# Graph convolution kernel: the bias of convolution 2 written into PSUM by ScalarE instead of added by TensorE

## The chip, the cores and the metric

One core of a Trainium2 chip runs the whole program. The time is the device time of one execution in microseconds; several executions are taken and their median is compared. One further execution is recorded by the hardware profiler, and every row below comes from it.

## What is computed

Three graph convolutions (GCN) over 30,000 nodes with 512 features and 30,000 edges, with layer norms, GELUs and residuals between them. Cut to what matters:

```python
h = relu(layernorm(x))                       # block 1 of the kernel
# x1 = x + L0(h):
r = h
h = gelu(layer_norm(gcn_conv(h, W1, b1), gamma1, beta1))       # convolution 1
h = layer_norm(gcn_conv(h, W2, b2), gamma2, beta2)             # convolution 2
x1 = x + gelu(h + r)
# x2 = x1 + L1(relu(layernorm(x1))):
out = x1 + gcn_conv(relu(layernorm(x1)), W3, b3)               # convolution 3

def gcn_conv(x, W, b):      # self loop added to every node, deg counts it
    # out[d] = sum over edges s->d of deg[s]^-1/2 deg[d]^-1/2 (x W)[s]  + b
```

## The kernel before

The 30,000 rows are worked on in 118 pairs of tiles (a pair is 256 rows, two tiles of 128 x 512, `j` = 0 and 1). The factor deg[s]^-1/2 is put on the rows before they are stored, and deg[d]^-1/2 is left out until later, so the bias enters each row as sqrt(deg) times b: a later layer norm or the last scaling takes the factor away again.

Block 1 counts degrees with one-hot products, normalises x, stores it to H0 and makes the index tables. Its VectorE queue is one written-out program; a ring of 14 buffers carries x in and H0 out. In it stand, for convolution 2 only: the transposed square roots of the degrees, split into a high and a low part (`sq_hi`, L432 to L434) and stored by SyncE to a table `SQ` in HBM (L286), and the operand `B3`, which holds b2 split the same way (L542 to L545). Tiles `root` of zeros, filled by GpSimd, are also the source of the zero rows written to H1 (L290).

Each convolution is one block that runs all pairs: the first four written out, then a hardware loop over four pairs a turn, then the last ones written out. Each engine has a `body(p, known)` that sets the order of its own queue; engines meet by semaphores. For a pair in convolution 2:

- SyncE: `load_self` (L797), `load_root` (L805, 3 rows of `SQ` for the pair), `load_x` (L817), `store_x` (L824, waits for `x2_sum`), `store_h` (L834, waits for `relu_x2`). The queue is in order: while it waits for `relu_x2`, the loads of the next body stand behind it.
- GpSimd: `residual` (L925), the gathers (L889), `power` (L932).
- TensorE: `aggregate(p+1)`: 8 transposes of the own rows (L1252), 8 of the gathered rows (L1259), 8 products of 256 columns (L1266); then `multiply_second(p)`: two bias products `root` x `B3` of 512 columns that open the two banks `Out` (L1296), and 24 products of 512 columns (L1275). The bias products wait for `cg_done` of two pairs before, that is until VectorE has read the banks (`centre`, L1117).
- VectorE: `over_low` (L1078, L1080), `low` (L1086, waits for ScalarE's `high`), `stats` of both tiles (L1094, each waits for its last product), mean and variance (L1103, L1110), `centre` (L1117), `x2_sum` of the pair before (L1144, waits for `relu_x2` of two pairs earlier, among others), `x2_mean` (L1152), `x2_scale` (L1165), `normal` (L1132), `x2_shift` (L1172), and in the loop the indices (L1072).
- ScalarE: `squares` (L1011, waits for `x2_mean`), `high` (L963), `gelu` (L979), `relu_x2` (L1021), `relu_x` (L1002, waits for the load of x), `over_high` (L957).

Convolutions 1 and 3 have no bias product. There ScalarE's `seed` (L972) writes sqrt(deg) times the bias into the bank, and `multiply` (TensorE) waits for `seeded` and then adds its products onto it.

Of the kernel before, what the change touches and what calls it, by code (L numbers as in the profile page):

```python
# [5 lines left out]
P = 128  # L6
ALU = mybir.AluOpType
ACT = mybir.ActivationFunctionType
F32 = mybir.dt.float32
# [46 lines left out]
def gnn_kernel(nc, x, src, dst, W1, b1, g1, be1, W2, b2, g2, be2, W3, b3, out):  # L56
# [19 lines left out]
    with ExitStack() as ctx:  # L76
# [45 lines left out]
        SQ = scratch("SQ", (NTE, 3 * P))  # L122
# [16 lines left out]
        sq_hi = sb("sq_hi", [P, 2, 3, P], F32R)  # L139
        B3 = sb("B3", [P, D], F32R)  # L140
# [23 lines left out]
        root = [sb(f"root{u}", [P, 2, P], F32R) for u in range(4)]  # L164
# [20 lines left out]
        b_hi, b_lo = Vhi[0][0:3, :], scratch_f[0:3, 4 * D:5 * D]  # L185
# [32 lines left out]
        roots, roots_turned, roots_made, roots_out = sem("roots"), sem("roots_turned"), sem("roots_made"), sem("roots_out")  # L218
# [29 lines left out]
        with nc.Block() as block:  # L248
            @block.sync
            def _(sp):  # L250
# [57 lines left out]
                sp.wait_ge(roots_out, 16 * len(THALF))  # L308
# [8 lines left out]
            def _(pool):  # L317
# [6 lines left out]
                for b in (B3, *(r[:, :, :] for r in root)):  # L324
                    nc.gpsimd.memset(b[...].bitcast(F32), 0.0).then_inc(consts, 1)
# [42 lines left out]
            def _(dve):  # L368
# [55 lines left out]
                nc.vector.tensor_tensor(sqrt_deg[:, :], deg1[:, :], dinv[:, :], ALU.mult).then_inc(roots, 1)  # L424
# [329 lines left out]
        def convolution(q):  # L754
# [30 lines left out]
            with nc.Block() as block:  # L785
                @block.sync
                def _(sp):
# [574 lines left out]
```

## Time and profile before

| | us |
|---|---|
| median of 3 runs | 3256.65 (3255.61 to 3258.55) |
| the profiled execution | 3256.22 |
| its span, first to last instruction | 3254.4 |
| TensorE busy in the span | 2927.4 (90%) |
| VectorE | 2558.2 (79%) |
| GpSimd | 2042.1 (63%) |
| ScalarE | 1917.1 (59%) |
| DMA, mean rate | 274 GB/s |

The profile names engines PE (TensorE matmul), PEld (its weight load), DVE (VectorE), ACT (ScalarE), POOL (GpSimd) and SP (SyncE). A trailing q is the engine's sequencer, which issues DMAs and waits. In the timeline a row is: start, length, engine, line, operation, output<-inputs, number of instructions merged, and in square brackets the idle time before it with what ended it. Instructions on one engine overlap a little, so a row's length is more than what it takes from the queue. The picture in slices of the page shows where the stages lie: block 1 to about 430 us, convolution 1 to about 1320, convolution 2 from there to about 2350, convolution 3 to the end.

### The profile page before, as it was taken

How to read it: one execution, taken by the hardware profiler on the slowest of the kernel's cores; microseconds unless marked ns; L12 is line 12 of the kernel's file. 1: busy time of each engine (PE TensorE's matmuls, PEld its weight loads, DVE VectorE, ACT ScalarE, POOL GpSimd, SP SyncE). 2: the span in 40 equal slices, each digit the busy share in tenths (PEclk: the TensorE clock that was granted, in tenths of full speed). 3: DMA queues.
4: the chain of work that ended last, by engine and by line, in shares of the span. 5: the costliest groups of instructions: out<-in, count | busy, mean ns of one | idle time of the engine just before them, and what ended most of it. 6: DMA issues, size and time to landing. Idle time of an engine off the chain costs nothing. (4 is left out here: it accounts for less than half of the span.)

```text
span 3254.4 us, 60981 instructions
## 1 busy us (share of the span) xinstructions
PE 2927.4 (90%) x16665; PEld 2468.1 (76%) x16665; DVE 2558.2 (79%) x6385; ACT 1917.1 (59%) x2847; POOL 2042.1 (63%) x1619
## 2 busy tenths in 40 slices
PE   8223359999999999899999999999969999999999
PEld 2122248888888888688888888888758888888888
DVE  9899968888888888699999999999934454454444
ACT  0256547767766776477777877777733333333333
POOL 0122257777777776588888888888655555555553
PEclk9999999999999999899999999999989999999999
DMA  3499987788888776699999999999789999999996
GB/s 130 157 355 418 416 253 213 213 216 219 214 216 218 214 215 175 225 322 331 323 328 328 322 331 323 327 326 326 262 236 287 287 289 291 285 288 287 288 289 208
DMA packets 306303, 890.91 MB, mean 274 GB/s; under 512 B 67591, under 2 KB 69033, under 8 KB 306248
## 3 DMA queue, kind: packets, MB, share of 16 engines
q1 hardware_dynamic: 190408, 682.26, 59.5%
q0 software_dynamic: 115840, 208.01, 27.1%
q8 instruction: 23, 0.38, 0.0%
q14 instruction: 32, 0.26, 0.0%
HBM read 653.10 MB, written 308.07 MB: 295 GB/s over the span
## 5 line engine op out<-in xcount | busy, mean ns | idle before, releaser
L889 POOL DMA_INDIRECT gathered<-H,idx x826 | 1154.7, 1398 | 517.0 <-issue 244.8
L1275 PE MATMUL out<-Whi,ahi 128*128 128x512 f32 x2832 | 765.6, 392 | 0.0
L1275 PE MATMUL out<-Wlo,ahi 128*128 128x512 f32 x2832 | 759.0, 390 | 0.0
L1275 PE MATMUL out<-Whi,alo 128*128 128x512 f32 x2832 | 739.3, 390 | 0.1
L963 ACT ACTIVATE ahi<-agg 128x1024 fp32r<-128x1024 f32 x354 | 361.0, 1020 | 642.1 <-PE agg L1266 586.4
L1275 PEld LDWEIGHTS out<-Wlo,ahi 128*128 128x128 f32 x2832 | 531.9, 188 | 115.7
L1275 PEld LDWEIGHTS out<-Whi,alo 128*128 128x128 f32 x2832 | 531.5, 188 | 110.9 <-DVE alo L1086 0.5
L1275 PEld LDWEIGHTS out<-Whi,ahi 128*128 128x128 f32 x2832 | 517.7, 189 | 97.3
L1078 DVE TENSOR_TENSOR vlo<-gathered,vhi 128x512 fp32r<-128x512 f32 x354 | 243.1, 687 | 320.7 <-ACT vhi L957 209.6
L1086 DVE TENSOR_TENSOR alo<-agg,ahi 128x1024 fp32r<-128x1024 f32 x354 | 429.7, 1214 | 24.0 <-ACT ahi L963 17.5
L1252 PE MATMUL agg<-ident,gathered 128*128 128x128 f32 x2832 | 370.0, 274 | 58.8 <-DMA gathered<-H,idx 49.0
L1094 DVE BATCH_NORM_STATS2 small<-out 128x6 f32<-128x512 f32 x472 | 327.0, 694 | 110.4 <-PE out L1275 77.1
L1252 PEld LDWEIGHTS agg<-ident,gathered 128*128 128x128 f32 x2832 | 331.9, 140 | 106.3 <-DMA gathered<-H,idx 50.7
L1266 PE MATMUL agg<-sv,vhi 128*128 128x256 f32 x1416 | 385.5, 305 | 1.7 <-DVE sv L1080 1.3
L925 POOL TENSOR_TENSOR r<-r,vec 128x512 f32<-128x512 f32 x236 | 298.8, 1286 | 99.3 <-DVE sv L1080 92.4
L1266 PE MATMUL agg<-sv,vlo 128*128 128x256 f32 x1416 | 356.5, 284 | 0.0
L979 ACT ACTIVATE y<-y 128x1024 f32<-128x1024 f32 x236 | 248.7, 1054 | 166.7 <-DVE y L1132 140.2
L1117 DVE SCALAR_TENSOR_TENSOR conv<-out,small,vec 128x512 f32<-128x512 f32 x472 | 331.3, 744 | 0.0
L972 ACT ACTIVATE out<-vec,sqrt_deg 128x512 f32<-128x512 f32 x472 | 306.0, 684 | 12.8 <-PEq L248 6.4
L932 POOL TENSOR_TENSOR small<-small,neg_half 128x2 f32<-128x2 f32 (+1 forms) x238 | 211.7, 889 | 151.9 <-DVE small L1110 140.2
L1181 DVE SCALAR_TENSOR_TENSOR conv<-out,dinv,x 128x512 f32<-128x512 f32 x236 | 176.6, 749 | 138.8 <-PE out L1275 119.7
L1266 PEld LDWEIGHTS agg<-sv,vhi 128*128 128x128 f32 x1416 | 272.7, 193 | 2.3 <-DVE vlo L1078 1.7
(176 smaller groups left out, 3824.2 us busy)
## 6 DMA issues: line engine op xcount, KB each, us to landing
gathered<-H SPq DMA_DIRECT2D x351, 512.0 KB
H<-ho SPq DMA_DIRECT2D x250, 512.0 KB, 9.5
x<-in_x_dram SPq DMA_DIRECT2D x165, 512.0 KB, 8.8
X<-x SPq DMA_DIRECT2D x117, 512.0 KB
x<-X SPq DMA_DIRECT2D x117, 512.0 KB
out_dram<-conv SPq DMA_DIRECT2D x117, 512.0 KB
H<-x SPq DMA_DIRECT2D x48, 512.0 KB, 9.6
gathered<-H,idx POOLq DMA_INDIRECT x826
```

Of the source, the lines that this page charges most:

```text
L889: pool.indirect_dma_start(rows, None, H[q][0:end, :], bass.IndirectOffsetOnAxis(ap=idx[p.slot(4)][:, c:c + 1], axis=0), bounds_check=end - ...
L925: nc.gpsimd.tensor_tensor(R[:, j, :], R[:, j, :], beta_b[1][:, :], ALU.add)\
L963: nc.scalar.activation(Ahi[p.slot(2)][:, :], Agg[p.slot(2)][:, :], ACT.Copy)\
L972: nc.scalar.activation(Out[2 * p.slot(2) + j][:, :], bias_b[q][:, :], ACT.Copy, scale=sqrt_deg[:, bass.ds(p.n * 2 + j, 1)]).then_inc(seede ...
L979: nc.scalar.activation(y, y, ACT.Gelu).then_inc(gelu_done.sem, 1)
L1078: nc.vector.tensor_tensor(Vlo[p.slot(2)][:, :], V[p.slot(4)][:, :], Vhi[p.slot(2)][:, :].bitcast(F32), ALU.subtract).then_inc(vlo_done.sem, 1)
L1086: nc.vector.tensor_tensor(Alo[p.slot(2)][:, :], Agg[p.slot(2)][:, :], Ahi[p.slot(2)][:, :].bitcast(F32), ALU.subtract).then_inc(lo_done.se ...
L1094: s = nc.vector.bn_stats(m[:, 6 * j:6 * j + 6], Out[2 * p.slot(2) + j][:, :])
L1117: nc.vector.scalar_tensor_tensor(CvP[p.slot(2)][:, j, :], Out[2 * p.slot(2) + j][:, :], m[:, 12 + 2 * j:13 + 2 * j], gamma_b[q][:, :], ALU ...
L1252: nc.tensor.matmul(agg[:, (2 * f + j) * P:(2 * f + j + 1) * P], own[:, j, fs], ident[:, :], is_transpose=True, start=(f % 2 == 0 and j == ...
L1266: m = nc.tensor.matmul(agg[:, 2 * f * P:2 * (f + 1) * P], part[p.slot(2)][:, f * P:(f + 1) * P], Sv[p.slot(2)][:, :], start=False, stop=(p ...
L1275: m = nc.tensor.matmul(Out[2 * p.slot(2) + j][:, :], a[p.slot(2)][:, c:c + P], w[q][:, f, :], start=False, stop=stop and f == KD - 1, skip ...
```

## The change

Convolution 2 gets its bias as the other two do: ScalarE's `seed` writes sqrt(deg) times b2 into both banks `Out` of a pair, and the two bias products are gone. `seed(p+2)` stands in ScalarE's body between `gelu(p)` and `relu_x2(p-2)`; the first two pairs are seeded ahead of the loop. TensorE waits for `seeded` (after its wait for `high`) in place of `cg_done` and of the root load. With the products go `B3`, `sq_hi`, the table `SQ`, its two stores and its 118 loads, the two transposes that turned the roots, and 12 small VectorE instructions in block 1. The zero rows of H1 come from a tile of their own, `zeros`.

```diff
-                nc.vector.tensor_scalar(row[:, 1:2], row[:, 0:1], 1.0, None, ALU.is_equal).then_inc(cols, 1)
-                dve.wait_ge(cols, 3)
-                link(nc.vector.tensor_scalar(row[:, 2:3], row[:, 1:2], -1.0, 1.0, ALU.mult, ALU.add))
...
-                sp.wait_ge(roots_made, 1)
-                for h, rows in THALF:
-                    sp.dma_start(SQ[h * P:h * P + rows, :], sq_hi[0:rows, h, :, :].bitcast(F32)
-                                 .rearrange("p a j -> p (a j)")).then_inc(roots_out, 16)
-                sp.wait_ge(consts, 6)
+                sp.wait_ge(consts, 2)
                 for k in range(2):
                     sp.dma_start(H[1][N:N + P, k * 2 * P:(k + 1) * 2 * P],
-                                 root[k][:, :, :].bitcast(F32).rearrange("p a j -> p (a j)")).then_inc(zero_out, 16)
+                                 zeros[:, :]).then_inc(zero_out, 16)
...
-                dve.wait_ge(roots_turned, 1)
-                for h, rows in THALF:
-                    r = slice(0, rows)
-                    nc.vector.tensor_copy(sq_hi[r, h, 0, :], bank[6 + h][r, 0:P])
-                    link(nc.vector.tensor_copy(sq_hi[r, h, 1, :], bank[6 + h][r, 0:P]))
-                    c = nc.vector.tensor_tensor(sq_hi[r, h, 2, :], bank[6 + h][r, 0:P], sq_hi[r, h, 0, :].bitcast(F32),
-                                                ALU.subtract)
-                c.then_inc(roots_made, 1)
...
-                dve.wait_ge(vectors_in, 16 * 7)
-                dve.wait_ge(consts, 6)
-                b = bias_b[1][0:3, :]
-                link(nc.vector.tensor_copy(b_hi, b))
-                link(nc.vector.tensor_tensor(b_lo, b, b_hi.bitcast(F32), ALU.subtract))
-                link(nc.vector.tensor_scalar(b_lo, b_lo, row[0:3, 1:2], None, ALU.mult))
-                link(nc.vector.scalar_tensor_tensor(B3[0:3, :], b_hi.bitcast(F32), row[0:3, 2:3], b_lo,
-                                                    ALU.mult, ALU.add))
...
-                pe.wait_ge(roots, 1)
-                for h, rows in THALF:
-                    m = nc.tensor.transpose(bank[6 + h][0:rows, 0:P], sqrt_deg[:, h * P:h * P + rows], ident[:, :])
-                m.then_inc(roots_turned, 1)
...
-                    def load_root(known, p, k):
-                        if not second:
-                            return
-                        if has(known, k - 4):
-                            sp.wait_ge(main_done.sem, main_done.upto(p.after(-4)))
-                        sp.dma_start(root[p.slot(4)][0:3, :, :].bitcast(F32), SQ[bass.ds(p.n * 2, 2), :]
-                                     .rearrange("o (a j) -> a o j", a=3)).then_inc(root_in.of(p), 16)
...
                         if has(known, 5):
                             load_self(known, p.after(5), 5)
-                        if has(known, 3):
-                            load_root(known, p.after(3), 3)
                         if has(known, 2):
                             load_x(known, p.after(2), 2)
...
                     def body(p, known):
                         if known == 0:
-                            if not second:
-                                seed(0, p)
+                            seed(0, p)
                             over_high(p)
...
                                 over_high(p.after(3))
+                                seed(1, p.after(1))
...
                             if has(known, 0):
                                 gelu(p)
+                            if has(known, 2):
+                                seed(of(known, 2), p.after(2))
                             if has(known, -2):
                                 relu_x2(of(known, -2), p.after(-2))
...
                     def multiply_second(p, known):
 
-                        pe.wait_ge(root_in.of(p), root_in.upto(p))
-                        for j in range(2):
-                            if known is None or known >= 2:
-                                pe.wait_ge(cg_done.sem, cg_done.upto(p.after(-2), j + 1))
-                            nc.tensor.matmul(Out[2 * p.slot(2) + j][:, :], root[p.slot(4)][:, j, :], B3[:, :],
-                                             start=True, stop=False, skip_group_check=True)
                         pe.wait_ge(hi_done.sem, hi_done.upto(p))
                         for j in range(2):
+                            pe.wait_ge(seeded.sem, seeded.upto(p, j + 1))
                             product(p, j, Ahi, Whi)
                             product(p, j, Ahi, Wlo)
```

ScalarE's queue in convolution 2, the last pair written out ahead of the loop, from `squares` to `over_high`. Before:

```order
L1011 ACTIVATE y,small<-x,small 128x512 x2
L963 ACTIVATE ahi<-agg 128x1024
L979 ACTIVATE y<-y 128x1024
L1021 ACTIVATE ho<-x,small 128x512 x2
L1002 ACTIVATE r<-x,nb_x,rstd_x 128x512 x2
L957 ACTIVATE vhi<-gathered 128x512
```

and now:

```order
L962 ACTIVATE y,small<-x,small 128x512 x2
L914 ACTIVATE ahi<-agg 128x1024
L930 ACTIVATE y<-y 128x1024
L923 ACTIVATE out<-vec,sqrt_deg 128x512 x2
L972 ACTIVATE ho<-x,small 128x512 x2
L953 ACTIVATE r<-x,nb_x,rstd_x 128x512 x2
L908 ACTIVATE vhi<-gathered 128x512
```

Two instructions more stand between `gelu` (L979, now L930) and `relu_x2` (L1021, now L972); all that follows them in the queue moves behind them.

SyncE's queue in convolution 2, the last body written out ahead of the loop: own rows, roots, x, the store of X2 and the store of H2. Before:

```order
L797 DMA gathered<-H 128x1024
L805 DMA root<-SQ 3x2x128
L817 DMA x<-in_x_dram 128x1024
L824 DMA X<-x 128x1024
L834 DMA H<-ho 128x1024
```

and now:

```order
L762 DMA gathered<-H 128x1024
L774 DMA x<-in_x_dram 128x1024
L781 DMA X<-x 128x1024
L791 DMA H<-ho 128x1024
```

The load of x now stands directly behind the load of the own rows; the waits between them are the same.

## Rows read from the trace of the kernel before

**Rows 1.** The page: busy time of each engine, its share of the span, instructions

```profile
PE 2927.4 (90%) x16665; PEld 2468.1 (76%) x16665; DVE 2558.2 (79%) x6385; ACT 1917.1 (59%) x2847; POOL 2042.1 (63%) x1619
```

**Rows 2.** Busy by stretch: stretch, length, busy (instructions) by engine, granted clock, DMA

```profile
200.00:400.00 200.00, 66.88 (x870) 45.77 (x870) 195.26 (x784) 121.06 (x167) 44.91 (x41) 1.00 1.02 415
...
1300.00:1400.00 100.00, 84.32 (x466) 73.01 (x464) 71.74 (x168) 53.46 (x81) 62.65 (x56) 0.90 0.72 241
...
1600.00:1800.00 200.00, 200.00 (x1157) 174.33 (x1156) 191.04 (x488) 158.49 (x257) 165.44 (x139) 1.00 0.94 326
```

**Rows 3.** Timeline of TensorE in convolution 2: bias products and those after

```profile
1700.73 0.63 PE L1296 MATMUL out<-B,root 128*128 128x512 f32 x2
1701.19 1.09 PE L1275 MATMUL out<-Whi,ahi 128*128 128x512 f32 x4
...
1709.37 0.63 PE L1296 MATMUL out<-B,root 128*128 128x512 f32 x2
```

**Rows 4.** Timeline of VectorE: `stats` of the first pair, then of two later ones

```profile
1344.12 1.28 DVE L1094 BATCH_NORM_STATS2 small<-out 128x6 f32<-128x512 f32 x2
...
1706.11 1.45 DVE L1094 BATCH_NORM_STATS2 small<-out 128x6 f32<-128x512 f32 x2
...
1714.64 0.69 DVE L1094 BATCH_NORM_STATS2 small<-out 128x6 f32<-128x512 f32 x1
1715.51 0.70 DVE L1094 BATCH_NORM_STATS2 small<-out 128x6 f32<-128x512 f32 x1 [0.18 <-PE out L1275]
```

**Rows 5.** Waits of ScalarE between 1450 and 2250 us: total, times, longest

```profile
ACT y L1011 <- DVE small L1152: 115.6, 89, 2.0
ACT r L1002 <- DMA x<-in_x_dram: 44.2, 69, 1.6
```

**Rows 6.** Timeline of ScalarE: a `seed` of convolution 1, a pair of convolution 2

```profile
1295.46 1.30 ACT L972 ACTIVATE out<-vec,sqrt_deg 128x512 f32<-128x512 f32 x2
...
1709.22 0.62 ACT L957 ACTIVATE vhi<-gathered 128x512 fp32r<-128x512 f32 x1
1711.03 0.72 ACT L1011 ACTIVATE y<-x,small 128x512 f32<-128x512 f32 x1 [1.19 <-DVE small L1152]
...
1714.31 1.51 ACT L1021 ACTIVATE ho<-x,small 128x512 f32<-128x512 f32 x2
1716.04 1.52 ACT L1002 ACTIVATE r<-x,nb_x,rstd_x 128x512 f32<-128x512 f32 x2 [0.22 <-DMA x<-in_x_dram]
```

**Rows 7.** Timeline: `relu_x2`, SyncE's loads behind it, `x2_sum`

```profile
1705.79 1.51 ACT L1021 ACTIVATE ho<-x,small 128x512 f32<-128x512 f32 x2
...
1708.68 0.29 SPq L805 DMA_DIRECT2D root<-SQ  x1
...
1709.24 0.32 SPq L817 DMA_DIRECT2D x<-in_x_dram  x1
...
1709.50 0.68 DVE L1144 SCALAR_TENSOR_TENSOR x<-x,y 128x512 f32<-128x512 f32 x1
```

**Rows 8.** Timeline: a late load of x, with the `relu_x2` ahead of it

```profile
1515.63 1.50 ACT L1021 ACTIVATE ho<-x,small 128x512 f32<-128x512 f32 x2
...
1519.88 0.33 SPq L817 DMA_DIRECT2D x<-in_x_dram  x1
...
1526.97 1.52 ACT L1002 ACTIVATE r<-x,nb_x,rstd_x 128x512 f32<-128x512 f32 x2 [1.21 <-DMA x<-in_x_dram]
```

**Rows 9.** Timeline of VectorE in block 1: around `sq_hi`, around `B3`

```profile
105.87 0.29 DVE L432 CAST sq_hi<-out 128x128 fp32r<-128x128 f32 x1 [0.37 <-PE out L607]
...
107.32 2.46 DVE L444 BATCH_NORM_STATS2 x_st<-conv 128x6 f32<-128x512 f32 x4
...
163.95 0.41 DVE L542 CAST vhi<-vec 3x512 fp32r<-3x512 f32 x1
...
166.40 2.47 DVE L444 BATCH_NORM_STATS2 x_st<-conv 128x6 f32<-128x512 f32 x4
```

**Rows 10.** Timeline of TensorE: transposes after a long idle time, before convolution 2

```profile
1322.36 1.97 PE L1252 MATMUL agg<-ident,gathered 128*128 128x128 f32 x8 [9.73 <-PEq L785]
```

More of the change, by code:

```diff
@@ L121, in gnn_kernel @@
         DST = scratch("dst_padded", (PADDED, 1), I32)
-        SQ = scratch("SQ", (NTE, 3 * P))
         ident = sb("ident", [P, P])
@@ L138, in gnn_kernel @@
         rstd_x, nb_x = sb("rstd_x", [P, NTE]), sb("nb_x", [P, NTE])
-        sq_hi = sb("sq_hi", [P, 2, 3, P], F32R)
-        B3 = sb("B3", [P, D], F32R)
         sqrt_deg = sb("sqrt_deg", [P, NTE])
@@ L163, in gnn_kernel @@
         idx = [sb(f"idx{u}", [P, 3], I32) for u in range(4)]
-        root = [sb(f"root{u}", [P, 2, P], F32R) for u in range(4)]
+        zeros = sb("zeros", [P, 2 * P])
         small = [sb(f"small{u}", [P, 36]) for u in range(4)]
@@ L184, in gnn_kernel @@
         fl = scratch_f[:, 3 * D:4 * D].rearrange("p (h j) -> p h j", h=2)
-        b_hi, b_lo = Vhi[0][0:3, :], scratch_f[0:3, 4 * D:5 * D]
         lo_t = sb("lo_t", [P, NC])
@@ L217, in gnn_kernel @@
         place_made, place_used = sem("places_made"), sem("places_used")
-        roots, roots_turned, roots_made, roots_out = sem("roots"), sem("roots_turned"), sem("roots_made"), sem("roots_out")
         w_split, w_free = sem("weights_split"), sem("weights_staged_free")
@@ L307, in _ @@
                     sp.dma_start(SelfP[n], whole(H[0], n, False)).then_inc(self_in.of(Pair(0, n)), 16)
-                sp.wait_ge(roots_out, 16 * len(THALF))
                 sp.wait_ge(vectors_in, 16 * 7)
@@ L323, in _ @@
                     nc.gpsimd.memset(m[:, :], 1.0)
-                for b in (B3, *(r[:, :, :] for r in root)):
-                    nc.gpsimd.memset(b[...].bitcast(F32), 0.0).then_inc(consts, 1)
+                nc.gpsimd.memset(zeros[:, :], 0.0).then_inc(consts, 1)
                 pool.wait_ge(padded, 48)
@@ L423, in _ @@
                 nc.vector.tensor_scalar(eps2[:, :], deg1[:, :], EPS, None, ALU.mult)
-                nc.vector.tensor_tensor(sqrt_deg[:, :], deg1[:, :], dinv[:, :], ALU.mult).then_inc(roots, 1)
+                nc.vector.tensor_tensor(sqrt_deg[:, :], deg1[:, :], dinv[:, :], ALU.mult)
                 dve.wait_ge(pair_cnts, 1)
@@ L740, in gnn_kernel @@
         g_self = sem("g_self")
-        root_in, xt_in = Landed("root_in", 4), Landed("xt_in", 4)
+        xt_in = Landed("xt_in", 4)
         ho_out, xo_out = Landed("ho_out", 2), Landed("xo_out", 2)
@@ L851, in fetch_x @@
                                 sp.wait_ge(xo_out.of(p), xo_out.upto(p))
-                            else:
-                                sp.dma_start(root[n][0:3, :, :].bitcast(F32), SQ[2 * n:2 * n + 2, :]
-                                             .rearrange("o (a j) -> a o j", a=3)).then_inc(root_in.of(p), 16)
                             sp.dma_start(XtP[n][:, :, :], whole(X2 if second else x, n, False)).then_inc(xt_in.of(p), 16)
@@ L860, in body @@
                                 load_self(0, p.after(k), k)
-                            load_root(0, p.after(2), 2)
                             load_self(0, p.after(4), 4)
@@ L1319, in convolution @@
             if second:
-                root_in.close()
                 for flag in (r_done, rb_done, x2_done, mean2_done, sq2_done, sc2_done, co2_done):
                     flag.close()
-            else:
-                seeded.close()
+            seeded.close()
             if third:
```

## The prediction

> **What bounds the kernel now.** I read the busy line of the page first, then the busy times by stretch, then the timeline of the engines in convolution 2, then the waits of ScalarE. TensorE is busy for 90% of the span [rows 1], and for all of the middle stretch of convolution 2 [rows 2]: 200.00 of 200.00 us. But there VectorE is busy for 191.04 of the same 200 us, and the DMA for 0.94 of them, so whatever TensorE gives back is capped soon. The pace of convolution 2 is TensorE's: from the bias products of one pair to those of the next 1709.37 - 1700.73 = 8.64 us [rows 3]. Of these the two bias products take 1701.19 - 1700.73 = 0.46 us; their row is 0.63 long because a matmul overlaps the next.
>
> How much slack has VectorE? It meets TensorE in one place, `stats`, which waits for the last products. In the first pair, where the products were long done, its two instructions took 1.28 us; later 1.45, and 1715.51 + 0.70 - 1714.64 = 1.57 [rows 4]. So VectorE waits for TensorE 0.17 to 0.29 us a pair, I take 0.22. Its own pace is then 8.64 - 0.22 = 8.42 us.
>
> ScalarE's slack: between 1450 and 2250 us, that is in 92.6 pairs, it waits 115.6 us for `x2_mean` and 44.2 us for the load of x [rows 5], 1.73 us a pair. Its own string is 8.64 - 1.73 = 6.91 us.
>
> **What the change does, part by part.**
>
> TensorE, convolution 2: two products fewer, 0.46 us a pair, pace 8.64 - 0.46 = 8.18 us. If TensorE stayed the bound, 118 x 0.46 = 54 us. It doesn't: VectorE's 8.42 is longer. So the most that a pair can give is 0.22 us, by the two ends of rows 4 0.17 to 0.29, times 117 steps 20 to 34 us, at 0.22 26 us.
>
> ScalarE, convolution 2: two `seed` instructions a pair. In convolution 1 such two take 1.30 us, the overlap with the next about 0.1, so 1.20 [rows 6]. ScalarE's string becomes 6.91 + 1.20 = 8.11 us, 0.31 under VectorE's 8.42. That is little. The Trainium skill (ScalarE: Activation LUTs, "Step-by-step: what each stage is for") says that ScalarE writes faster into PSUM than into SBUF. The rows don't agree: a 512-wide copy into SBUF takes 0.62, and of two seeds into PSUM each 0.65 or more. By the page the two seeds would cost at most 2 x 0.62 - 0.1 = 1.14, and the slack would be 0.37 in place of 0.31; the time would be some 1 us lower.
>
> The new wait, TensorE for `seeded`: queued behind it are the 24 products of the pair, and for those wait `stats` and all behind it. The seeds of a pair are issued where `relu_x2` starts now, 1714.31 [rows 6], and end 1.3 us later, 1715.6. The products of their pair follow the bias products at 1709.37 + 8.64 = 1718.01 [rows 3]. 2.4 us to spare, so this wait costs nothing in the loop. At the start the seeds stand in ScalarE's idle time before the first gather has landed, nothing either.
>
> What stands behind the seeds in ScalarE's queue: `relu_x2` is done 1.20 later. Two wait for it. VectorE's `x2_sum` starts at 1709.50, the `relu_x2` it needs ends at 1705.79 + 1.51 = 1707.30 [rows 7]: of 2.20 us 1.00 is left, 0.8 at the faster pace. And SyncE's store and, behind it, the next load of x.
>
> **The loop through the load of x** is the part that decides. From the end of `relu_x2` 1707.30 SyncE issues the store, the own rows, the roots (1708.68), and at 1709.24 x; `relu_x` starts at 1716.04 after a wait for it [rows 6, 7]. That is 8.74 us after the end of `relu_x2`, 6.80 of it from issue to use. In a late case `relu_x2` ends at 1517.13, x is issued at 1519.88 and used at 1526.97: 9.84 us, 7.09 from its issue [rows 8]. On the mean ScalarE waits 44.2 / 92.6 = 0.48 us there [rows 5], so x comes about 8.64 + 0.48 = 9.12 after `relu_x2`. Without the root load the issue is 1709.24 - 1708.68 = 0.56 earlier: 8.56 on the mean, 9.28 in the late case. From the start of `relu_x` to the end of the `relu_x2` that closes the loop, ScalarE needs `relu_x` and `over_high`, 1.52 + 0.62 less overlaps = 2.0, from `squares` to the end of `relu_x2` 1714.31 + 1.51 - 1711.03 = 4.79, and now 1.20 for the seeds: 8.0 us. The loop spans two pairs. On the mean it takes 8.56 + 8.0 = 16.56, 8.28 a pair, under VectorE's 8.42. In a late case 17.28, which is 0.44 over two of VectorE's pairs. Reading along the timeline, about one load in four is late like this. When it is, `squares` starts late, then `high`, then VectorE's `low`: I take 0.3 us for one pair in four, 0.08 a pair. Pace 8.50.
>
> 117 x (8.64 - 8.50) = 16.4 us gained in convolution 2.
>
> Block 1: `sq_hi` holds VectorE from 105.87, after a wait of 0.37, to 107.32, 1.8 us; `B3` from 163.95 to 166.40, 2.45 us [rows 9]. VectorE is busy 195.26 of the 200 us that follow [rows 2], so both lie on the path; against it, the DMA share there is 1.02. Bounds 0 and 4.3, I take 4, nearer to VectorE's row. The stores of `SQ` and the memsets of `root` go from queues that wait there anyway: nothing. Convolution 3 and convolution 1 are as they were: nothing.
>
> Sum: 16.4 + 4 = 20.4 us. The profiled execution took 3256.22 and becomes 3235.8; the median of the runs is 0.4 above it, so 3236.
>
> **The rivals.** *VectorE's pace in full*: no late load is felt, 8.42 to 8.35 a pair. 26 to 34 us and 4.3: 3226 down to 3218. For it: the root loads are off the queue; against it the thin slack of ScalarE. Its upper part belongs to my case.
>
> *ScalarE takes TensorE's place*: late loads are the rule, 17.28 / 2 = 8.64 a pair. Nothing is gained in convolution 2, and 0 to 4 in block 1: 3252 to 3257. For it: ScalarE's slack falls from 1.73 to 0.3 us, and at a quicker pace the DMA, at 0.94, is pressed harder. Against it: the same DMA moves 415 GB/s in block 1 and 326 here [rows 2].
>
> *Slower, the load of x comes later still*: with `relu_x2` later, x falls into the gathers of GpSimd. The loop is longer than 2 x 8.64 as soon as x takes 17.28 - 8.0 = 9.28 us after `relu_x2` on the mean and not 8.56, 0.72 more. If it took 1.2 us more, (9.76 + 8.0) / 2 = 8.88 a pair, 117 x 0.24 = 28 us lost, 4 gained: 3280.
>
> *Slower by the clock*: after 9.73 idle us eight transposes took 1.97 us [rows 10], and the granted clock of that stretch is 0.90, a mix of 1.2 and 2.4 GHz [rows 2]. In convolution 2 TensorE would idle 8.50 - 8.18 = 0.32 us a pair, which it does not now. At 1.2 GHz a pair would need 16.4 us, so 6% of the time at that clock is enough to be slower than now; 15% would be 8.18 x 1.15 = 9.4 a pair, +89 us, 3342. Against it: in block 1 TensorE is busy 66.88 of 200 us at a clock of 1.00 [rows 2]. The Trainium skill (TensorE: Matmul & The Clock Gate, "A second HAM failure mode: psum-queue depth-cycling") warns of such short idle times between groups of matmuls; by block 1 they do no harm here.
>
> *The change doesn't do what it says*: VectorE turns out faster than I read and the full 54 us come: 3198.
>
> **How the numbers follow.** Chances: my case, 3226 to 3249, 0.60; VectorE's pace in full, 0.12; the full 54 us 0.02; ScalarE in TensorE's place 0.16, of it 0.02 still faster; the load of x 0.07; the clock 0.01; something in the start or the end of a block that I don't see, 0.02, slower. About 0.2%, 6.5 us, is what a measurement of this kernel can tell from no change. Faster 0.76, same 0.14, slower 0.10. Predicted 3236; the range for 8 in 10 goes from 3222, inside VectorE's pace in full, to 3257, where nothing is gained.
>
> **What would show it.** Right: no L1296; the pace of convolution 2 between 8.42 and 8.60; VectorE's `stats` back at 1.28 us with no wait for TensorE; TensorE idle about 0.3 us a pair, in front of the products or of the transposes; ScalarE's wait for `x2_mean` fallen from 1.25 to some tenths, at times none; block 1 some 4 us shorter. Wrong: VectorE's `low` waiting for `high` in most pairs (ScalarE is the bound); x used more than 7.6 us after its issue; a granted clock under 1.00 between 1400 and 2300; convolution 1 or 3 changed in length.

## The result, and the profile after

| | before | after |
|---|---|---|
| median of 6 runs each, us | 3256.2 (3254.8 to 3258.6) | 3271.7 (3266.3 to 3275.2) |
| ratio, with its 95% interval | | 1.0046 (1.0036 to 1.0057) |
| span of the profiled execution | 3254.4 | 3270.8 |
| first to last product of convolution 1 | 859.0 | 858.3 |
| first to last product of convolution 2 | 1013.8 | 1032.6 |
| first to last product of convolution 3 | 858.4 | 858.1 |

The forecast was 3236 and faster; the kernel is 15 us slower. Convolution 1 begins 2.5 us earlier, convolutions 1 and 3 take what they took, and convolution 2 takes 18.8 us more. Here and below the pace of convolution 2 is the mean distance between the starts of VectorE's first `centre` of one pair and of the next, over some 90 pairs between 1440 and 2250 us. It was 8.64 us before, the same as in [rows 3], and is 8.83 after.

The busy line of the page after, to be read beside [rows 1]:

```profile
PE 2904.5 (89%) x16427; PEld 2433.2 (74%) x16427; DVE 2548.5 (78%) x6373; ACT 2053.4 (63%) x3083; POOL 2062.6 (63%) x1615
```

and the stretch from the middle of convolution 2, with the columns of [rows 2] (busy us and instructions of PE, PEld, DVE, ACT, POOL, then clock, DMA share, GB/s):

```profile
1600.00:1800.00 200.00, 190.61 (x1083) 162.92 (x1082) 185.57 (x474) 179.60 (x294) 165.85 (x135) 0.99 0.94 317
```

TensorE was busy for 200.00 of these 200 us and is now for 190.61; VectorE fell from 191.04 to 185.57, and the DMA from 326 to 317 GB/s. ScalarE rose from 158.49 to 179.60 and isn't full either; GpSimd stayed where it was (165.44, now 165.85). No engine is the bound: a chain that passes through several of them is. The waits between 1450 and 2250 us (total us, times, longest) name it:

```profile
ACT r L953 <- DMA x<-in_x_dram: 64.4, 64, 2.8
...
PE out L1228 <- ACT out L923: 31.2, 44, 1.6
DVE alo L1039 <- ACT ahi L914: 26.3, 41, 1.4
...
ACT y L962 <- DVE small L1105: 11.6, 28, 0.7
```

Beside [rows 5]: ScalarE's wait for `x2_mean`, its slack, fell from 115.6 to 11.6 us. Its wait for the load of x rose from 44.2 to 64.4, and there are two waits that were not there before: TensorE waits for the seeds, and VectorE's `low` for ScalarE's `high`. VectorE waits for TensorE nowhere, so its `stats` are back at the length that [rows 4] shows for the first pair, as forecast.

One turn of the chain, from the timeline of ScalarE and of SyncE's queue (start, length, engine, line, operation):

```profile
1701.68 1.51 ACT L972 ACTIVATE ho<-x,small 128x512 f32<-128x512 f32 x2
...
1703.36 0.35 SPq L791 DMA_DIRECT2D H<-ho  x1
...
1704.12 0.35 SPq L762 DMA_DIRECT2D gathered<-H  x1
...
1704.78 0.34 SPq L774 DMA_DIRECT2D x<-in_x_dram  x1
...
1712.68 1.52 ACT L953 ACTIVATE r<-x,nb_x,rstd_x 128x512 f32<-128x512 f32 x2 [0.27 <-DMA x<-in_x_dram]
...
1718.03 1.29 ACT L923 ACTIVATE out<-vec,sqrt_deg 128x512 f32<-128x512 f32 x2
1719.26 1.51 ACT L972 ACTIVATE ho<-x,small 128x512 f32<-128x512 f32 x2
```

`relu_x2` ends at 1703.19. SyncE issues the store, the own rows, and at 1704.78 the load of x. `relu_x` had to wait for it and starts at 1712.68, 9.49 us after the end of `relu_x2` and 7.90 after the issue. The `relu_x2` that ends this turn is done at 1720.77, 8.09 later: 17.58 us for two pairs, 8.79 a pair. On the mean of the stretch x is issued 1.54 us after the end of `relu_x2` and used 7.99 after that, 9.53 together. With ScalarE's 8.0 us that is 17.53, 8.77 a pair.

What a late x does to the others stands in two rows of the same pair, VectorE's `low` and TensorE's first products:

```profile
1699.64 1.22 DVE L1039 TENSOR_TENSOR alo<-agg,ahi 128x1024 fp32r<-128x1024 f32 x1 [1.36 <-ACT ahi L914]
...
1701.18 1.19 PE L1228 MATMUL out<-Whi,ahi 128*128 128x512 f32 x4 [1.46 <-ACT out L923]
```

### The profile page after: what moved, and what is told of

Its sections match the earlier page's. It is cut to its first block and busy times, and to the rows that moved or that the text cites. A ratio compares the mean times of both kernels' runs of the same rounds, so it can differ in the third digit from the quotient of the medians.

```text
span 3270.8 us, 60605 instructions
## 1 busy us (share of the span) xinstructions
PE 2904.5 (89%) x16427; PEld 2433.2 (74%) x16427; DVE 2548.5 (78%) x6373; ACT 2053.4 (63%) x3083; POOL 2062.6 (63%) x1615
## 5 line engine op out<-in xcount | busy, mean ns | idle before, releaser
L1228 PE MATMUL out<-Whi,ahi 128*128 128x512 f32 x2832 | 778.9, 397 | 39.8 <-ACT out L923 38.5
L1228 PEld LDWEIGHTS out<-Whi,ahi 128*128 128x128 f32 x2832 | 509.9, 189 | 146.0 <-ACT out L923 50.9
L923 ACT ACTIVATE out<-vec,sqrt_deg 128x512 f32<-128x512 f32 x708 | 458.0, 681 | 16.4 <-PEq L750 9.8
L1047 DVE BATCH_NORM_STATS2 small<-out 128x6 f32<-128x512 f32 x472 | 315.2, 688 | 99.0 <-PE out L1228 99.0
L930 ACT ACTIVATE y<-y 128x1024 f32<-128x1024 f32 x236 | 248.8, 1054 | 163.0 <-DVE y L1085 162.9
```

The source lines that it names most:

```text
L923: nc.scalar.activation(Out[2 * p.slot(2) + j][:, :], bias_b[q][:, :], ACT.Copy, scale=sqrt_deg[:, bass.ds(p.n * 2 + j, 1)]).then_inc(seede ...
L930: nc.scalar.activation(y, y, ACT.Gelu).then_inc(gelu_done.sem, 1)
L1047: s = nc.vector.bn_stats(m[:, 6 * j:6 * j + 6], Out[2 * p.slot(2) + j][:, :])
L1228: m = nc.tensor.matmul(Out[2 * p.slot(2) + j][:, :], a[p.slot(2)][:, c:c + P], w[q][:, f, :], start=False, stop=stop and f == KD - 1, skip ...
```

## The experiments

**Is it the loop through the load of x? Open it, before and after.** The first two runs load x a body earlier, in the changed kernel and in the kernel before (this edit and those below are for convolution 2 alone):

```diff
                         if has(known, 5):
                             load_self(known, p.after(5), 5)
-                        if has(known, 2):
+                        if second and known == 0:
+                            load_x(0, p.after(2), 2)
+                        if not second and has(known, 2):
                             load_x(known, p.after(2), 2)
...
                         if has(known, -1):
                             store_x(known, p.after(-1), -1)
+                        if second and has(known, 3):
+                            load_x(known, p.after(3), 3)
                         if has(known, -lag):
                             store_h(known, p.after(-lag), -lag)
```

> The changed kernel with one reorder in SyncE's queue of convolution 2: the load of x for the next body but two is issued right behind the store of X2, ahead of the store of H2, so that it no longer waits for relu_x2. Theory A (the loop relu_x2 -> store -> load of x -> relu_x -> relu_x2 sets the pace of 8.83 us): the loop is cut, VectorE's own 8.42 to 8.45 us becomes the pace, 117 x 0.39 = 46 us less than the changed kernel's 3271.7, so 3224 to 3229, clearly under the kernel before; ScalarE doesn't wait for x. Theory B (ScalarE's own string with the seeds is too long): no gain from the reorder, 3268 to 3273. Theory C (TensorE's new wait for the seeds, or its clock): no gain either.

> The kernel before with the same reorder of the load of x. Theory A: TensorE sets the pace there (8.64 us), the wait for x was covered, so 3256 within 2 us; only ScalarE's wait for x goes and its wait for x2_mean grows by as much. If the load of x had cost something before too, it would be faster.

Measured: e1 3241.7 us, ratio to before 0.9957 (0.994 to 0.9973), pace 8.57. e2 3255.6, 1.0001 (0.9991 to 1.001), pace 8.64. The same edit takes 30 us from the changed kernel and nothing from the one before. ScalarE's wait for x is gone from the waits of e1. So waiting behind the load of x is what makes the changed kernel slow, and it cost the one before nothing. e2 came as forecast; e1 missed its 3224 to 3229 by 13 us, for it stops at 8.57 and not at the 8.42 of the prediction. That is the second question, taken up below.

**Or get `relu_x2` out of the seeds' way, or x out of the own rows' way.** e3 keeps all loads where they are and moves the seeds behind `relu_x2`:

```diff
                             if has(known, 0):
                                 gelu(p)
+                            if has(known, -2):
+                                relu_x2(of(known, -2), p.after(-2))
                             if has(known, 2):
                                 seed(of(known, 2), p.after(2))
-                            if has(known, -2):
-                                relu_x2(of(known, -2), p.after(-2))
```

> The changed kernel with seed(p+2) behind relu_x2(p-2) in ScalarE's queue and not ahead of it; SyncE's order as in the change. The seeds then fill the time in which ScalarE waits for the load of x. Theory A (the loop through the load of x): the seeds are out of the loop, 9.5 + 6.8 us in two pairs, so VectorE's 8.57 is the pace: 3241 to 3244, as the two kernels at 3241. Theory B (it is the sum of ScalarE's work that is too much): the sum is the same, so 3268 to 3274. Against A as far as TensorE needs the seeds: they end 1.5 us later, of 2.4 us that there were.

e6 issues the load of x ahead of that of the own rows:

```diff
+                        if second and has(known, 2):
+                            load_x(known, p.after(2), 2)
                         if has(known, 5):
                             load_self(known, p.after(5), 5)
-                        if has(known, 2):
+                        if not second and has(known, 2):
                             load_x(known, p.after(2), 2)
```

> The changed kernel with the load of x ahead of the load of the own rows in SyncE's queue of convolution 2; it still stands behind the store of H2. A dose between the change and the load ahead of that store. Theory A: x is issued 0.7 us earlier and with 512 KB less ahead of it, which is worth 1.5 us or more of the 9.5 after relu_x2: the loop falls under two of VectorE's pairs, pace 8.57, 3241 to 3245. If x comes when it came, whatever the order of issue, 3268 to 3274.

Measured: e3 3239.6 us, 0.9955 (0.9938 to 0.9971); e6 3241.4, 0.9955 (0.9939 to 0.9972). e6 lies in its forecast and e3 1.4 us under its own. Three different ways to shorten the loop, one place where they stop. In e3 the seeds run while ScalarE waits for x anyway, so they cost nothing. In e6 x is used 8.47 us after `relu_x2` and not 9.53, and in only one of 94 pairs does ScalarE still wait for it.

**Both remedies together.**

> The changed kernel with both remedies of the first runs: the load of x a body earlier, and the seeds behind relu_x2. Theory L (the loop through the load of x sets the changed kernel's pace, and behind it stands VectorE's own pace of 8.57 us): either remedy alone already reaches VectorE's pace, so both together give no more than one: 3239 to 3242 us, pace 8.55 to 8.57. Rival S (each remedy takes a share of a cost of its own): 3239.6 less some 10 us, under 3232.

3241.2 us, 0.9957 (0.994 to 0.9973), pace 8.56: no more than one alone.

**The seeds alone, and no bias at all.** e4 is the kernel before with the seeds added: the bias products stay and open the banks, which discards what the seeds wrote, and TensorE waits for the seeds. e5 is the changed kernel without seeds and without b2; the first product of a tile opens its bank.

> The kernel before with ScalarE's two seeds a pair added in convolution 2, in the place where the change has them, and nothing taken away: the bias products stay and overwrite the seeds, and wait for them. Theory A (the delay of relu_x2 by 1.2 us is the whole cause): the pace is 8.8 us or, since the root load still stands ahead of the load of x, up to 9.1; with block 1 as before 3256 + 117 x (0.2 to 0.45) = 3279 to 3308. Theory C (TensorE loses its full load, its clock or its start-up after a wait): TensorE still has all its products, so close to 3256.

> The changed kernel with no bias at all in convolution 2: neither seeds nor bias products, the first product opens the bank. b2 is left out of the result. This is the saving alone, without its price. Theory A: ScalarE is as it was, TensorE at 8.18 us, so VectorE's 8.42 is the pace: 3256.2 - 117 x 0.22 - 2.5 (block 1) = 3228. If VectorE's own pace was misread, it shows here: 3200 if TensorE stays the bound, 3250 or more if something else is.

e4: 3269.6 us, 1.0048 (1.0031 to 1.0064), pace 8.73. e5: 3241.3, 0.9958 (0.9941 to 0.9974), pace 8.57. Neither came as forecast. e4 lies between the 3256 of theory C and the 3279 from which theory A began: the seeds alone do make the kernel before slower, and there x comes 9.32 us after `relu_x2`, which by the loop is (9.32 + 8.0) / 2 = 8.66 a pair. e5 stops at 8.57 like e1 and not at 8.42. Seen from e5, the change is a gain of 15 us, for the products and all that came with them, and a loss of 30 us for the seeds where they stand.

**The dose.** e9 writes one seed a pair (tile 1 gets no bias), e11 writes a third tile between the two seeds, into SBUF, for nobody. e12 is e11 with the load of x a body earlier.

```diff
                         for j in range(2):
+                            if second and j == 1:
+                                if known is None or known >= 1:
+                                    act.wait_ge(third_done.sem, third_done.upto(p.after(-1)))
+                                nc.scalar.activation(extra[:, :], bias_b[q][:, :], ACT.Copy)\
+                                    .then_inc(third_done.sem, 1)
```

> Half the dose: in convolution 2 only tile 0 of a pair is seeded, tile 1 has no bias (b2 is left out of it) and its first product opens the bank. Theory L: ScalarE's part of the loop is 8.0 - 0.6 = 7.4 us, x comes 9.2 to 9.5 us after relu_x2, so the loop is 16.6 to 16.9 over two pairs, 8.3 to 8.45 a pair, under VectorE's 8.57; only late loads are felt: pace 8.57 to 8.68, 3242 to 3255 us. Rival P (each seed costs by its own length, or by taking the PSUM bank from VectorE or TensorE): half way between no seeds, 3241.3, and two seeds, 3271.7: 3256.5.

> More of the dose: between the two seeds of a pair ScalarE writes a third 128x512 tile, into an SBUF tile that nobody reads; the result is the same. Theory L: ScalarE's part of the loop is 8.6 us in place of 8.0, 0.6 over two pairs, 0.3 a pair: 8.83 + 0.30 = 9.13, 35 us more than the change, 3306; at the slower pace the DMA is less pressed and x may come up to 0.3 us sooner, so 3290 to 3307. Rival P (the seeds cost by writing into PSUM while VectorE or TensorE use it): a write into SBUF costs nothing of it, 3272. Rival A (ScalarE's own string, without the loop, is what bounds): 8.11 + 0.6 = 8.7, still under 8.83: 3272.

> The same third write, with the load of x a body earlier, so that the loop is open. Theory L: the next bounds are VectorE's 8.57 and ScalarE's own string, 8.11 + 0.6 = 8.7 us: pace 8.6 to 8.75, 3243 to 3262 us, some 45 under the run with the third write alone. Rival (a longer ScalarE string costs without the load of x, through squares, high and low): about the time of the run with the third write alone, 3290 or more.

| writes a pair, loop closed | 0 (e5) | 1 (e9) | 2 (after) | 3 (e11) | 3, loop open (e12) |
|---|---|---|---|---|---|
| median, us | 3241.3 | 3249.6 | 3271.7 | 3292.5 | 3242.3 |
| pace, us | 8.57 | 8.62 | 8.83 | 8.98 | 8.57 |

Ratios to before: e9 0.9983 (0.9973 to 0.9992), e11 1.0118 (1.0101 to 1.0135), e12 0.9959 (0.9945 to 0.9973). The first write costs 8 us, each further one some 21: the shape of a loop that comes over another bound. A loop that were the only bound would pay 0.6 / 2 x 117 = 35 us a write, so it isn't alone in the changed kernel; what else is at work comes below. The third write goes into SBUF and costs as much as a second seed, so it isn't PSUM that is short. With the loop open the same three writes cost nothing (e12 is even just under its forecast), though ScalarE then has hardly a free moment. The stretch of e12:

```profile
1600.00:1800.00 200.00, 198.31 (x1120) 168.81 (x1119) 194.66 (x493) 197.84 (x328) 175.37 (x141) 1.00 0.96 329
```

ScalarE is busy for 197.84 of 200 us, at the pace of e1. A full engine outside the loop costs less than one that is busy for 179.60 us inside it.

**The root loads.** e8 keeps the tables, the root loads and TensorE's wait for them, but has seeds and no bias products. e17 is e8 with each root load behind the load of x. e18 is the changed kernel with a small load for nobody ahead of each load of x.

> The kernel before with the seeds added and the bias products taken out, but everything else kept: sq_hi, B3 and the table are made, and the roots are loaded for each pair, and waited for, though nothing reads them. It lies between the kernel before with the seeds (pace 8.73) and the changed kernel (8.83). If the root load between the own rows and x does no harm to x, as the kernel without any bias suggests (x comes 9.2 us after relu_x2 there, as before): 3268 to 3276. If the missing root load is what makes x late in the change: 3262 to 3268. If the root load costs its 0.56 us, as predicted: 3290 or more.

> The kernel with seeds and root loads kept, but each root load stands behind the load of x in SyncE's queue and not ahead of it. Theory O (the small load ahead holds back the issue of x by 0.65 us, and x lands the sooner after its issue for it, since it then falls less into other transfers): x is issued 1.5 us after relu_x2 as in the changed kernel, takes 8.0 to its use, the pace goes from 8.70 to about 8.83, 3264.1 + 14 = 3278, at least 3271. Rival P (it is the presence of the small loads that helps, wherever they stand): 3262 to 3267.

> The changed kernel with a small load (3 rows of 1 KB, for nobody) put ahead of each load of x in convolution 2, where the root load was. Theory O: x is issued some 2.2 us after relu_x2 and used 7.0 to 7.2 later, pace 8.70, convolution 2 14 us shorter: 3271.7 - 14 = 3258, 3255 to 3262. Rival X (the difference between the changed kernel and the one with the root loads kept lies elsewhere, for instance in TensorE's wait for the roots): 3269 to 3276. Rival P gives the same here as theory O.

| | after | e8 | e17 | e18 |
|---|---|---|---|---|
| a small load stands | nowhere | ahead of x | behind x | ahead of x |
| median, us | 3271.7 | 3264.1 | 3266.3 | 3264.4 |
| range of the runs | 3266.3 to 3275.2 | 3259.3 to 3269.3 | 3262.3 to 3268.5 | 3259.8 to 3271.1 |
| end of `relu_x2` to issue of x | 1.54 | 2.24 | 1.50 | 2.21 |
| issue of x to its use | 7.99 | 7.00 | 7.96 | 7.26 |
| pace | 8.83 | 8.69 | 8.77 | 8.80 |

Ratios to before: e8 1.0029 (1.0018 to 1.0041), e17 1.0031 (1.0019 to 1.0044), e18 1.0027 (1.0016 to 1.0037). Two things are plain. A small load ahead of x puts off its issue by 0.7 us, and x takes 0.7 to 1.0 us less from there to its use. Taking the root loads out made nothing quicker. Whether it made the kernel slower is open. e8 came out in the range that blames the missing root load, 3262 to 3268. In e17 x behaved as theory O says, but the time, 3266.3, lies in the range of rival P and not at 3271 or more; e18 gave half of the 14 us of theory O and P and lies in no range. All three kernels with small loads, wherever these stand, are 5 to 8 us under the changed one. The intervals of the four ratios meet, and kernels whose loop is closed differ by 6 to 11 us from one execution to the next.

Why an earlier issue brings nothing can be read from the trace after. The stores and loads of SyncE share one queue, which moves 238 GB/s between 1450 and 2250 us (243 before), while the DMA engines are busy for 0.94 of the time. In 23 turns the landings of both the own rows and x are recorded: x is issued 0.66 us behind the own rows and lands 1.9 us behind them on the mean. So it seems that x lands when the bytes ahead of it have gone, and a load of 3 KB less ahead of it takes next to none away. e6 issues x 0.77 us sooner and takes 512 KB away from ahead of it, and there x does come at least 1 us sooner. This is a reading of traces; no run was made for it.

**Why VectorE stops at 8.57.** In the open kernels a small instruction of VectorE, `x2_var_eps`, takes 0.49 us in place of 0.25. The groups of VectorE instructions between 1450 and 2250 us show it, before and in e1 (count, busy us, mean ns, idle before):

```profile
L1159 DVE SCALAR_TENSOR_TENSOR small<-small,eps_c 128x2 f32<-128x2 f32 x92 | 22.6, 246 | 0.0
```

```profile
L1116 DVE SCALAR_TENSOR_TENSOR small<-small,eps_c 128x2 f32<-128x2 f32 x94 | 45.8, 488 | 0.0
```

It stands between `stats` and the two aggregations. e10 is e1 with it ahead of `stats`:

> The changed kernel with the load of x ahead of the store of H2, and besides x2_var_eps moved from between stats and the aggregation to ahead of stats in VectorE's queue of convolution 2. In the kernels whose pace VectorE sets, that 2-column row is 0.49 us long, before 0.25. If the length is its own cost, the pace falls from 8.57 to about 8.35 and the time from 3241.7 to 3215 or so. If VectorE just can't start the aggregation sooner after stats, the time between them stays at 1.0 us, the small instruction costs its 0.1 to 0.2 elsewhere, and the time is 3241 to 3255.

e10: 3259.8 us, 1.0012 (1.0003 to 1.0022), pace 8.74, slower than e1 by 18 us and outside both forecasts. The row is still 426 ns long there, and the aggregation now stands directly behind `stats`, for whose end it waits. So the length isn't a matter of what runs ahead of it on VectorE. What then? GpSimd. The timeline of e1, GpSimd's `residual` (two additions of 128 x 512, both inputs in SBUF) and `x2_var_eps`:

```profile
1705.63 2.53 POOL L880 TENSOR_TENSOR r<-r,vec 128x512 f32<-128x512 f32 x2 [0.28 <-DVE sv L1037]
```

```profile
1706.50 1.28 DVE L1051 BATCH_NORM_STATS2 small<-out 128x6 f32<-128x512 f32 x2
1707.70 0.48 DVE L1116 SCALAR_TENSOR_TENSOR small<-small,eps_c 128x2 f32<-128x2 f32 x1
1708.10 0.23 DVE L1060 BATCH_NORM_AGGREGATE small<-small 128x2 f32<-128x6 f32 x2
```

GpSimd's additions end at 1705.63 + 2.53 = 1708.16, `x2_var_eps` at 1707.70 + 0.48 = 1708.18. In all 94 pairs of e1 it ends 13 to 24 ns behind them, in all 92 of the kernel before 16 to 26 ns behind them. In the changed kernel it has the choice: in 26 pairs the additions are over when it starts, and it takes 143 ns; in the other 65 it takes 386. In e10 it starts early and ends with the first of the two additions:

```profile
1711.22 1.29 POOL L880 TENSOR_TENSOR r<-r,vec 128x512 f32<-128x512 f32 x1 [0.98 <-DVE sv L1037]
```

```profile
1712.12 0.41 DVE L1116 SCALAR_TENSOR_TENSOR small<-small,eps_c 128x2 f32<-128x2 f32 x1
```

1712.51 and 1712.53. The price is in the order too: from the start of `x2_var_eps` to that of `var_eps` it is 1714.27 - 1712.12 = 2.15 us, in e1, from the start of `stats`, 1708.47 - 1706.50 = 1.97, 0.18 a pair more. `stats`, with one input in PSUM, and `low`, with one in PSUM and one in SBUF, run over the same additions at their usual length: `low` takes 1207 ns on the mean in e1, and 1207 in convolution 1 of the kernel before, where GpSimd adds nothing. The Trainium skill (GPSIMD Engine Reference, section "1. Specifications") says that GpSimd's way to SBUF is shared with VectorE, and that they contend where a VectorE instruction has two SBUF inputs. These rows agree: `x2_var_eps` has two, and is held until the GpSimd instruction under way is done. But not every pair of such instructions does this. `x2_sum` has two inputs in SBUF as well and starts while GpSimd works on `power` (128 x 4), in e1:

```profile
1709.37 1.04 POOL L887 TENSOR_TENSOR small<-small,neg_half 128x4 f32<-128x4 f32 x1
1709.87 0.68 DVE L1101 SCALAR_TENSOR_TENSOR x<-x,y 128x512 f32<-128x512 f32 x1
```

`power` is under way until 1710.41, and `x2_sum` takes 0.68 us, as it does when `power` isn't running. What is shown is the hold by the large additions.

Four runs test it. e14 is e1, e15 the kernel before, e16 the changed kernel, each with the addition cut to 128 of its 512 columns, so the rest of beta1 is left out. e13 is e1 with `x2_var_eps` behind the aggregations and nothing left out:

```diff
+                        if second and has(known, 0):
+                            mean_var(p)
                         if second and has(known, -2):
                             v = x2_var_eps(p.after(-2))
...
                         if has(known, 0):
-                            mean_var(p)
+                            if not second:
+                                mean_var(p)
                             var_eps(p)
                             centre(p)
```

> The kernel with the early load of x, and x2_var_eps moved from ahead of the two aggregations to behind them, in convolution 2. Theory G (GpSimd's residual addition holds up a VectorE instruction whose two inputs are both in SBUF, until it ends): the aggregations have one input, pass, and x2_var_eps comes when the addition is over. From the second stats to var_eps it is now 0.60 + 0.41 + 0.37 = 1.38 us, start to start; it becomes the 0.82 that stats to aggregation took with x2_var_eps out of between, 0.37 to 0.5 on, 1.2 to 1.3 in all: 0.08 to 0.18 a pair, 10 to 21 us, so 3221 to 3232. x2_var_eps's row goes from 488 ns to under 250. Rival T (the instruction is long whatever stands around it): row over 400 ns, 3241 or more.

> The kernel with the early load of x, and GpSimd's residual addition cut to the first 128 of 512 columns (the rest of beta1 is left out). Theory G: the addition is over before x2_var_eps starts, its row is near 143 ns, VectorE's own pace is the 8.42 us of the prediction (8.57 - 0.15), 3241.7 - 117 x 0.15 = 3224; 3215 to 3228. Rival T: row stays near 488 ns, 3240 to 3243.

> The kernel before with the same short residual addition. There TensorE sets the pace at 8.64 us, and x2_var_eps takes 246 ns, so the hold is hidden behind TensorE: both theories give 3252 to 3256. Were it under 3245, VectorE and not TensorE would bound the kernel before.

> The changed kernel with the same short residual addition. If the loop through the load of x is what bounds it, VectorE's hold has little part in it: 3262 to 3273. Rival (the changed kernel is slow because VectorE is held by GpSimd): the 15 us and the gain of the change come at once, under 3240.

| | e13 | e14 | e15 | e16 |
|---|---|---|---|---|
| median, us | 3227.9 | 3222.9 | 3255.2 | 3257.6 |
| ratio to before | 0.9912 (0.9896 to 0.9929) | 0.9897 (0.9881 to 0.9914) | 0.9999 (0.999 to 1.0009) | 1.0008 (0.9998 to 1.0017) |
| mean of `x2_var_eps`, ns | 138 | 142 | 144 | 143 |
| pace | 8.44 | 8.39 | 8.64 | 8.73 |

The hold is real and worth 19 us where VectorE is the bound (e1 to e14), nothing where TensorE is (e15). A short addition also frees GpSimd for its gathers; e13 leaves GpSimd as it is and brings 14 of the 19 us. e16 fell out of its range, 3262 to 3273, downwards: 14 us of the changed kernel's time are also due to the hold, though ScalarE still waits for x there. In the changed kernel both are at work, the loop in some pairs and VectorE in others. The rival, that the hold explains it all, needed under 3240.

VectorE's rows in e13, its queue in the new order:

```profile
1710.31 1.28 DVE L1051 BATCH_NORM_STATS2 small<-out 128x6 f32<-128x512 f32 x2
1711.73 0.25 DVE L1060 BATCH_NORM_AGGREGATE small<-small 128x2 f32<-128x6 f32 x2
1711.91 0.16 DVE L1116 SCALAR_TENSOR_TENSOR small<-small,eps_c 128x2 f32<-128x2 f32 x1
1712.12 0.20 DVE L1067 TENSOR_TENSOR small<-small,eps 128x2 f32<-128x2 f32 x1
```

The aggregations have one input and pass under the addition; when `x2_var_eps` comes, it is nearly over. From the start of `stats` to that of `var_eps` it is 1.81 us, in e1 1.97 (1706.50 to 1708.47). e13 computes all that the reference asks and beats both kernels, by 28 us and by 44.

## Why the prediction was wrong, point by point

**TensorE gives back 0.46 us a pair, and is then not the bound.** Right. It is busy for 190.61 of 200 us, and even with the bias gone altogether (e5) the pace is not TensorE's 8.18 but 8.57.

**VectorE's own pace is 8.42.** Wrong as it was worked out, and right in a kernel without the hold (e14 8.39; e13, which steps out of it, 8.44). The step took VectorE's wait for TensorE, 0.22 us, off the pace of 8.64, as if what comes behind the wait would move up by as much. But `x2_var_eps` can't end before GpSimd's additions, and these start from VectorE's `sv` ahead of `low`, not from `stats`. Without the wait ahead of `stats`, `x2_var_eps` starts earlier and takes 0.49 in place of 0.25. What is left of 0.22 is 0.07: e1, e3, e5, e6 and e7 all stand at 8.56 to 8.57. A wait had hidden a hold.

**Two seeds cost ScalarE 1.20 us a pair, 8.11 in all.** Right in size: from 1718.03 to 1719.26 the two take 1.23. The sum of 8.11 is somewhat high: with a third write on top it would be 8.7, and e12 keeps 8.57. The Trainium skill (ScalarE: Activation LUTs, "Step-by-step: what each stage is for") says that ScalarE writes faster into PSUM than into SBUF. The prediction held that the rows don't agree, but it compared a seed, which has a scale for each row, with a copy that has none. The same instruction with such a scale stands in convolution 1 of the kernel before, `ho<-y,dinv` (L991), from SBUF into SBUF: its rows are 716 ns long, those of a seed into PSUM 684. These rows agree with the skill, by some 30 ns.

**The wait for `seeded` costs nothing, 2.4 us to spare.** Wrong in the kernel as it came out, 31.2 us of waiting in 44 pairs; but as a sequel. ScalarE is late by then, from x. Where x is early the 2.4 us aren't there either: TensorE, no longer the bound, runs ahead until it meets the seed. In e1 its weight loads wait for the seed in 92 of the 94 pairs, 25.2 us in all. That costs nothing, for e5, without seeds, has the same pace.

**The loop through the load of x takes 8.56 + 8.0 us.** This is the step that failed. ScalarE's 8.0 held (8.09 in the turn shown). The other term was 9.12 in the kernel before (2.19 + 6.98 = 9.17 as measured), less 0.56 because the root load no longer stands ahead of x. The issue did come earlier, by 0.65 (2.19 to 1.54), and x was used no sooner: 9.53 after, and 9.21 in e5, which has neither seeds nor root loads. The prediction had moved the landing with the issue. The runs show that the landing doesn't follow: with a small load ahead of x or without it, x comes 9.2 to 9.5 us after `relu_x2` (e8, e17, e18, after). By the trace it seems to be the bytes ahead of it in the queue that hold it; no run has tested that.

**The pace 8.50, by 0.08 for late loads.** Late loads are no exception that costs 0.08, they are the rule; [rows 5] already had ScalarE waiting for x 69 times in some 93 pairs, and not in one of four. The pace is 8.83 in place of 8.50, and in convolution 2 a loss of 18.8 us where a gain of 16.4 was forecast.

**Block 1 gives 4 us.** About right. Its end can be read from TensorE's first product of convolution 1, at 453.59 us before and 451.10 after. 2.5 us here; in the experiments on the changed kernel it comes at 448.8 to 451.4, against 453.0 to 453.7 where block 1 is the old one, so some 3.5 on the mean.

**The rivals.** The slower one named the right mechanism and the right threshold: slower as soon as x takes more than 9.28 us after `relu_x2`. It took 9.53. By its own rule that is (9.53 + 8.0) / 2 = 8.77 a pair and 15 us lost in convolution 2. It had only 0.07, because the sum had taken the shorter queue of SyncE for a sooner x. "ScalarE takes TensorE's place" reckoned with the same loop at 8.64 a pair; the two together had 0.23 and were one case, a loop with 0.1 us a pair to spare and a term known to 0.6. The clock did no harm: it is 0.99 in the stretch in which TensorE idles 9.4 of 200 us, and 0.91 between 1300 and 1400 us, where it was 0.90.

Of the signs of being wrong that the prediction had set out, one spoke plainly: x is used 7.99 us after its issue, and the limit was 7.6. The other, `low` waiting for `high` in most pairs, came in part: 26.3 us, in 41 of some 91 pairs.

## What to carry to other kernels

Work moved to an engine with idle time is only free if it isn't put into a loop: look for what is queued behind it whose end releases a load, and add the load's whole time, issue to use, to the engine's string. A load that is issued sooner behind the same bytes need not land sooner. Put such work where the engine waits for that load anyway; here the same two seeds cost 30 us ahead of `relu_x2` and nothing behind it. And when a wait is taken off a queue, look at what the next instructions run beside, on other engines too, before the whole wait is booked as a gain.

## What the runs showed of the hardware

- A VectorE instruction of 128 x 2 elements with both inputs in SBUF takes 0.14 us by itself. If it starts while GpSimd adds 128 x 512 tiles in SBUF, it ends 13 to 26 ns behind the GpSimd instruction under way, here up to 0.50 us after its start; if it starts in the last 0.11 us of an addition it just takes its 0.14. `low` and `stats`, with an input in PSUM, and the aggregations, with one input, are not held by these additions, and `x2_sum`, with two inputs in SBUF, is not held by GpSimd's `power` of 128 x 4.
- A 512 KB load that is issued 0.65 us earlier, because a load of 3 rows ahead of it is gone, lands no earlier; its time from issue to use goes from 6.98 to 7.99 us in the changed kernel and to 7.67 in e5. In the trace after, x lands 1.9 us behind the own rows, which are issued 0.66 us ahead of it. That the bytes ahead of it hold it is read from this and from e6, not tested.
- ScalarE's copy of 128 x 512 with a scale for each row takes 684 ns a row into PSUM and 716 into SBUF.
- Kernels in which this loop sets the pace spread by 6 to 11 us from run to run, those bound by VectorE by 1 to 3, except e3 with 8; e9 and e10, between the two, by 4.
